# A recommendation tower on one core: dense layers with samples on partitions, last block in two groups, weight preparation moved

## The chip, the cores and the metric

The kernel runs on one core of one Trainium2 chip. The metric is the device time of one execution in microseconds (us). Engines: TensorE (PE in the rows; PEld its weight loads), VectorE (DVE), ScalarE (ACT), GpSimd (POOL), and the sync engine (SP), which here only issues transfers; "SPq", "ACTq" are the queues of these engines. All arithmetic is in float32.

## The reference, cut to what matters

For each of 512 samples 26 rows of 64 numbers are gathered from tables (`e`); `r_dense_t` is 512 x 256. EPS is 1e-5, NI is 33, gains and shifts are inputs.

```python
x = layer_norm(dense_t @ Wd.T, gd, bd)                          # 512 x 128
y = layer_norm(jnp.einsum('bnd,ed->bne', sparse_t, Ws), gs, bs) # 26 x 128 a sample
y = jnp.einsum('bne,pn->bep', y, Wsi)                           # 26 -> 32
y = layer_norm(y, gsi, bsi)
T = jnp.concatenate([x[:, None, :], jnp.swapaxes(y, 1, 2)], axis=1)   # 33 x 128
Z = jnp.einsum('bnd,bmd->bnm', T, T)
Zflat = Z[:, TRIL_I, TRIL_J]                                    # 528 a sample
out = layer_norm(Zflat @ Wl.T, gl, bl)                          # 512, first 384 kept
h = jnp.concatenate([z, r_dense_t], axis=1)
h = jnp.maximum(h @ W_top1 + b_top1, 0.0)                       # 640 -> 512
h = jnp.maximum(h @ W_top2 + b_top2, 0.0)                       # -> 256
y = h @ W_top3                                                  # -> 1
```

## The kernel before

**Tiling.** The 512 samples are four blocks of 128 (`BLOCKS`), each of four units of 32 samples (`BU`); 16 units in all. One step `step(t)` handles unit t. Each engine has its instructions in an order written out by hand; semaphores tie them together, and an engine that waits holds back all that stands behind the wait.

**A step.** GpSimd gathers the table rows (L257): 104 indirect transfers in a fixed order, two for each slot of `g_sb` (13 slots a block; a unit takes the next 4, 3, 3, 3 slots). On TensorE: `mix(t)` (L299) needs the scaled rows of unit t; `transposes(t + 1)` (L273) needs the gathered rows of unit t + 1; `project(t)` (L318) needs the copy `U` (ScalarE, L600, `keep_u`) of what mix made; `norms(t + 1)` (L284); `inner(t - 1)` (L333), the products of the 33 vectors. VectorE then adds the bias (L831), forms the norms of unit t + 1 and scales its rows (L802 to L824), which releases `mix(t + 1)`, and makes `T` (L850). ScalarE copies, squares, takes roots, and at the end of the step moves `psZ` to `Zs` in four pieces of 32 partitions (L639, `keep_z`), behind which stands the next `keep_u`.

**Layers behind a block.** When four units are in `Zs`, the sync engine moves them to `Zt` by seven transfers (`relay`, L214), so that 127 pairs lie on partitions, in 5 columns. The layers then have features on partitions: `linear` (L352) multiplies 4 x 5 weight tiles of 128 x 128 by `Zt` (128 samples), `variance` (L366) sums squares with a matrix of ones, `layer1` (L372) is 12 products, `layer2` (L409) 8, `output` (L417) 2. VectorE divides `psH` by the deviation and adds the part of layer 1 from the dense input, `hd` (L864 to L881). These are dealt to steps 6 to 15 (`LINEAR` is 6; `linear` is cut at `EARLY`). The last block's layers run behind step 15 (L424 to L469), its second half of `Zs` having been moved by seven transfers from the queues of SP, ScalarE and GpSimd.

**Weights.** `hd` for all 512 samples is 8 products of 512 columns (`dense_part`, L479): two parts before the first gathered rows are turned, the third before step 0, the fourth in step 0. The linear weights `wl` (1280 KB) are loaded once slot 3 is there (L226), summed on ScalarE in steps 1 and 2 (L749), scaled in steps 4 and 5 (L754); in steps 5 to 8 a bias is added to `hd` (L766).

## Time and profile before

| | us |
|---|---|
| time, median of 3 executions (lowest, highest) | 303.85 (299.91, 304.52) |
| span of the profiled execution | 185.4 |
| TensorE busy | 148.0 |
| VectorE busy | 130.1 |
| ScalarE busy | 106.9 |
| GpSimd busy (gathers) | 104.3 |
| mean granted clock of TensorE | 0.936 |

The time counts more than the span from the first to the last instruction: at the median 303.85 - 185.4 = 118.45 us lie around it. Busy times overlap, since the engines work side by side; which of them sets the pace has to be read step by step. The page's chain of waits, followed back from the last instruction, gives 40% of the span to TensorE, 23% to ScalarE, 19% to VectorE and 11% to issue.

### The profile page before, as it was taken

The numbers are of one execution on the slowest core, as the hardware profiler recorded it, in microseconds if no ns is written. First come the engines' busy times: TensorE is split into PE (matmuls) and PEld (weight loads), VectorE is DVE, ScalarE is ACT, GpSimd is POOL, SyncE is SP. The second block draws the span as 40 slices with busy tenths as digits, with TensorE's granted clock in tenths as the row PEclk, the third lists the DMA queues.
The fourth block names the chain that finished last, engine by engine and source line by source line (L and its number), as shares of the span: only waits on it lengthen the run. The fifth ranks groups of instructions, "written<-read, shape, count | busy, mean of one in ns | idle before, by whom it ended". The sixth has DMA issues, their size and how long they took to land.

```text
span 185.4 us, 4668 instructions
## 1 busy us (share of the span) xinstructions
PE 148.0 (80%) x1825; PEld 113.2 (61%) x1825; DVE 130.1 (70%) x300; ACT 106.9 (58%) x245; POOL 104.3 (56%) x111
## 2 busy tenths in 40 slices
PE   0089877977969947459996978899799799977995
PEld 0084544434549544419794947569596666877994
DVE  6269659772959594908697999579799967943142
ACT  1202435594868486866667877585877857831230
POOL 3778777877878777777777777777840000020000
PEclk9999999996999669855999999999999999997899
DMA  5816334141111112311111123111111100110000
GB/s 153 294 33 194 137 58 161 32 139 26 34 21 29 24 28 61 61 27 27 28 33 23 32 58 64 28 28 25 28 25 40 33 7 11 27 38 0 0 0 0
DMA packets 6003, 9.59 MB, mean 52 GB/s; under 512 B 2303, under 2 KB 3538, under 8 KB 5854
## 3 DMA queue, kind: packets, MB, share of 16 engines
q0 software_dynamic: 3392, 3.45, 10.3%
q1 hardware_dynamic: 2232, 5.08, 9.1%
q10 hardware_dynamic: 358, 0.78, 1.1%
q8 instruction: 14, 0.23, 0.5%
q14 instruction: 7, 0.06, 0.1%
HBM read 8.01 MB, written 0.00 MB: 43 GB/s over the span
## 4 chain that ended last, share of the span: by engine, by line
PE 40%; ACT 23%; DVE 19%; issue 11%; DMA 5%; ACTq 1%; DVEq 0%
PE psB L318 11%; ACT Zs L639 10%; DVE B L831 4%; ACT U L600 4%; DMA dense_sb<-in_dense 4%; PE psG L284 4%; DVE qA L809 4%; DVE prod L802 3%; PE psZ L333 3%; PE psW L352 3%; PE psU L299 3%; DVE ssB L838 3%; ACT sdB L617 2%; PE psB L520 2%; PE psZ L424 2%
## 5 line engine op out<-in xcount | busy, mean ns | idle before, releaser
L257 POOL DMA_INDIRECT g_sb<-in_table,row_id x104 | 102.8, 989 | 31.7 <-issue 31.4
L831 DVE TENSOR_TENSOR B<-psB,bias 128x512 f32<-128x512 f32 x31 | 20.0, 686 | 26.2 <-PE psB L318 26.2
L639 ACT ACTIVATE Zs<-psZ 32x264 f32<-32x264 f32 x59 | 36.3, 616 | 2.1 <-PE psZ L333 1.0
L318 PE MATMUL psB<-U,ws_g 64*128 64x512 f32 x64 | 20.9, 735 | 15.3 <-ACT U L600 15.2
L611 ACT ACTIVATE sqB<-B 128x512 f32<-128x512 f32 x31 | 19.1, 632 | 23.1 <-DVE B L831 23.1
L299 PE MATMUL psU<-wsi_x,g_sb 128*128 128x192 f32 (+4 forms) x128 | 23.3, 330 | 7.3 <-DVE g_sb L824 7.3
L299 PEld LDWEIGHTS psU<-wsi_x,g_sb 128*128 128x128 f32 x128 | 20.9, 206 | 11.1 <-DVE g_sb L824 11.0
L284 PEld LDWEIGHTS psG<-gram,sT 128*128 128x128 f32 x104 | 14.0, 207 | 14.5 <-ACT sT L587 10.0
L850 DVE TENSOR_TENSOR T<-B,rB 128x512 f32<-128x512 f32 x31 | 21.5, 692 | 1.1
L838 DVE TENSOR_REDUCE ssB<-sqB 128x16 f32<-128x512 f32 x32 | 21.7, 677 | 0.1
L284 PE MATMUL psG<-gram,sT 128*128 128x128 f32 x104 | 17.2, 308 | 0.7 <-ACT sT L587 0.7
L318 PEld LDWEIGHTS psB<-U,ws_g 64*128 64x128 f32 x64 | 5.4, 208 | 20.0 <-ACT U L600 20.0
L214 POOL DMA_DIRECT2D Zt<-Zs x2 | 1.1, 549 | 26.5 <-ACT Zs L639 26.5
L333 PE MATMUL psZ<-T 128*32 128x33 f32 x960 | 13.0, 202 | 0.3 <-issue 0.2
L333 PEld LDWEIGHTS psZ<-T 128*32 128x32 f32 x960 | 10.8, 112 | 3.3 <-issue 1.6
L352 PE MATMUL psW<-Zt,wl_g 127*128 127x128 f32 x100 | 12.8, 286 | 0.0
L352 PEld LDWEIGHTS psW<-Zt,wl_g 127*128 127x128 f32 x100 | 12.1, 199 | 0.5 <-issue 0.4
L600 ACT ACTIVATE U<-psU 128x512 f32<-128x512 f32 x16 | 9.5, 595 | 2.5 <-PE psU L299 2.2
L802 DVE TENSOR_TENSOR prod<-psG,g_sb 128x384 f32<-128x384 f32 (+1 forms) x16 | 9.3, 583 | 2.1 <-PE psG L284 2.1
L594 ACT ACTIVATE sdA<-qA,eps_c 128x6 f32<-128x6 f32 (+1 forms) x16 | 4.8, 300 | 9.5 <-DVE qA L812 9.0
L824 DVE TENSOR_TENSOR g_sb<-g_sb,rA 128x384 f32<-128x384 f32 (+1 forms) x16 | 9.5, 592 | 0.6
L809 DVE TENSOR_REDUCE qA<-prod 128x6 f32<-128x384 f32 (+1 forms) x16 | 9.4, 586 | 0.6
(159 smaller groups left out, 226.7 us busy)
## 6 DMA issues: line engine op xcount, KB each, us to landing
g_sb<-in_table,row_id POOLq DMA_INDIRECT x104, 2.5
wl_sb<-in_wl SPq DMA_DIRECT2D x1, 1280.0 KB, 6.0
w_sb<-in_w SPq DMA_DIRECT2D x2, 512.0 KB, 5.4
w_sb<-in_w SPq DMA_DIRECT2D x1, 768.0 KB, 4.5
small_sb<-in_small SPq DMA_DIRECT2D x1, 615.5 KB, 4.1
dense_sb<-in_dense ACTq DMA_DIRECT2D x1, 512.0 KB, 7.3
Zt<-Zs SPq DMA_DIRECT2D x3, 80.0 KB
Zt<-Zs SPq DMA_DIRECT2D x3, 70.0 KB
```

The source lines that it names most:

```text
L257: pool.indirect_dma_start(g_sb[:, k, h * DSP:(h + 1) * DSP], None, table, bass.IndirectOffsetOnAxis(row_id[:, 2 * k + h:2 * k + h + 1], 0) ...
L284: mm = pe.matmul(psG[:, n * P:(n + 1) * P], sT[:, u % 2, n * P:(n + 1) * P], gram[:, :], start=True, stop=True)
L299: mm = pe.matmul(psU[:, (lo - US * j) * PROJ:(hi - US * j) * PROJ], g_sb[:, SLOTS * b + c, :], wsi_x[:, c, lo - s0:hi - s0, :], start=(n = ...
L318: pe.matmul(psB[h][:, :], ws_g[h * DSP:(h + 1) * DSP, :], U[h * DSP:(h + 1) * DSP, u % 2, :], start=not (last and h == 0), stop=True).then ...
L333: mm = pe.matmul(bank[gq * PROJ:(gq + 1) * PROJ, n * COLS:(n + 1) * COLS], T[:, u % 2, h, s, 2:2 + PROJ], T[:, u % 2, h, s, 0:COLS], start ...
L352: mm = pe.matmul(bank[:, at * BS:(at + 1) * BS], wl_g[0:KL, jj, f * P:(f + 1) * P], Zt[0:KL, b, :, jj, :], start=(jj == 0), stop=(jj == CW ...
L600: act.activation(U[:, u % 2, :], psU[:, :], ACT.Copy).then_inc(U_ready, 1)
L611: act.activation(sqB[:, h, :], at, ACT.Square).then_inc(B_squared, 1)
L639: act.activation(to, product, ACT.Copy).then_inc(Z_kept, 1)
L831: dve.tensor_tensor(B[:, h, :].rearrange("p (s j) -> p s j", j=PROJ), psB[h][:, :].rearrange("p (s j) -> p s j", j=PROJ), bias[:, :].rearr ...
L838: dve.tensor_reduce(ssB[:, h, :], sqB[:, h, :].rearrange("p (s j) -> p s j", j=PROJ), AX, ALU.add).then_inc(B_summed, 1)
L850: dve.tensor_tensor(T[:, u % 2, h, :, 2:], at.rearrange("p (s j) -> p s j", j=PROJ), rB[:, h, :].rearrange("p (s o) -> p s o", o=1).broadc ...
```

## The change

Rows and lines of after are those of the changed kernel.

1. **Samples on partitions.** `linear`, layer 1 and layer 2 now take the activations as the stationary operand and stream the weights: 5 products of 512 columns, 3 of 512, 4 of 256. For this the activations are turned on TensorE twice (`turn_z`, 3 transposes; `turn_h`, 4), each behind a copy on ScalarE (`keep_zc`, `keep_zT`, `relu_h`). The squares are summed by the accumulator of the squaring itself (`square_z`), so `variance` goes; the deviation is one number a partition. VectorE computes h1 = hd x sd + product in one instruction (`add_h1`), likewise h2 (`add_h2`), multiplies by the last weights with an accumulator (in place of `output`), and divides at the end (`finish_y`).
2. **Last block as two groups of 64 samples.** A group's product is split by columns into two halves that write partitions 0 to 63 and 64 to 127 (`GROUPS`, g = 2); the halves are added by a product with `same_sb` (`fold`, `fold_y`). The first group's transfers start when units 12 and 13 are in `Zs`, the second's after unit 15, three from SP and four from GpSimd each (`SP_RELAYS`, `POOL_RELAYS`).
3. **Dense part.** One part for each block, in steps 4, 5, 9 and 13 (`HD_STEPS`), with its bias as a further product; each copy by ScalarE stands in the step behind it.
4. **Weights.** `wl` is loaded as soon as the dense input is there, and summed on ScalarE before step 0; it is scaled in steps 1 to 3. The first weights of layer 1 (768 KB) are loaded once slot 5 is there (before: slot 7), the dense ones (512 KB) once slot 8 is there (before: at the start). `late` (448 KB) is a new input, loaded after slot 14. The x part (`xn`, `xT`) moves behind the first unit's norms and into step 0.
5. **Output.** Five transfers of 4 bytes from each partition in place of one of 2 KB from one partition.

```diff
+HD_STEPS = (4, 5, 9, 13)
+GROUPS = ((0, 1), (1, 1), (2, 1), (LAST, 2), (LAST, 2))
```

SP's queue:

```diff
+            sp.wait_ge(d_dense, 16)
+            sp.dma_start(wl_sb[:, :, :], wl).then_inc(d_wl, 16)
+            sp.wait_ge(gathered[5], 32)
+            sp.dma_start(w1_sb[:, 0:KZ, :], w1[:, 0:KZ, :]).then_inc(d_w1, 16)
+            sp.wait_ge(gathered[8], 32)
             sp.dma_start(w1_sb[:, KZ:, :], w1[:, KZ:, :]).then_inc(d_w1d, 16)
-            sp.wait_ge(gathered[3], 32)
-            sp.dma_start(wl_sb[:, :, :], wl).then_inc(d_wl, 16)
```

TensorE: linear, the transposes, layer 1, the folding, and the step:

```diff
-            def linear(b, lo, hi):
+            def linear(k, lo=0, hi=CW):
...
-                for n in range(lo, hi):
-                    f, jj = n // CW, n % CW
-                    bank, at = (psW, f) if b < LAST - 1 else (psW_third[f // 2], f % 2)
-                    mm = pe.matmul(bank[:, at * BS:(at + 1) * BS], wl_g[0:KL, jj, f * P:(f + 1) * P],
-                                   Zt[0:KL, b, :, jj, :], start=(jj == 0), stop=(jj == CW - 1))
-                if hi == ALL or b == LAST - 1:
...
+                for jj in range(lo, hi):
+                    for n in range(g):
+                        mm = pe.matmul(psL[k][n * s:(n + 1) * s, 0:w], zt_of(k)[0:KL, jj, :], wl_g[0:KL, jj, n * w:(n + 1) * w],
+                                       start=(jj == 0), stop=(jj == CW - 1))
+                if hi == CW:
                     mm.then_inc(W_done, 1)
...
+            def turn_z(k):
+                g = GROUPS[k][1]
...
+                for c in range(KZ if g == 1 else 2):
+                    mm = pe.transpose(psQ[k][:, c * P:(c + 1) * P], zc[:, c * P:(c + 1) * P], eye_sb)
+                mm.then_inc(ztr_done, 1)
...
+                        mm = pe.matmul(psF[k][n * s:(n + 1) * s, 0:w], zT[:, place(c, g)],
+                                       w1_g[:, c, n * w:(n + 1) * w], start=(c == 0), stop=(c == KZ - 1))
+                if hi == KZ:
...
+            def fold(k):
+                pe.wait_ge(z_squared, k + 1)
...
+                pe.matmul(psS[k][:, 0:1], same_sb, ssq[:, k:k + 1], start=True, stop=True).then_inc(folded, 1)
...
                 mix(t)
+                if t == UNITS - 2:
+                    linear(b, 0, 2)
                 if t + 1 < UNITS:
                     transposes(t + 1)
+                if late_step and j == 1 and t < UNITS - 1:
+                    turn_z(b)
+                if late_step and j == 2:
+                    turn_h(b)
                 project(t)
                 if t + 1 < UNITS:
                     norms(t + 1)
-                if late and j == 1 and t < UNITS - 1:
-                    linear(b, EARLY[b], ALL)
+                else:
+                    turn_z(b)
                 if t:
                     inner(t - 1)
-                if t == UNITS - 1:
-                    linear(b, EARLY[b], ALL)
                 if t == 0:
-                    dense_part(3)
+                    x_part()
                 if t == 1:
+                    shift_part(0, 3)
+                if t == 2:
+                    shift_part(3, CW)
                     x_sum()
-                    shift_part(0, 2)
-                if t == 2:
-                    shift_part(2, CW)
                 if t == 3:
                     bias_part()
-                if late and j == 0:
-                    if b:
-                        output(b - 1)
-                    linear(b, 0, EARLY[b])
-                if late and j == 1 and t < UNITS - 1:
-                    variance(b)
-                if late and j == 2:
-                    layer1(b)
-                if late and j == 3:
+                if t in HD_STEPS:
+                    dense_part(HD_STEPS.index(t))
+                if late_step and j == 0:
+                    linear(b, 2 if t == UNITS - 2 else 0, CW)
+                if late_step and j == 1 and t < UNITS - 1:
+                    top1(b)
+                if late_step and j == 2:
                     layer2(b)
```

What stands behind the last step on TensorE in the changed kernel is shown by its order below. ScalarE, new functions and the step (keep_hd is dealt behind rows_out, the weights' scaling to the step's end):

```diff
+            def keep_zc(k):
+                n = FOUT if k < LAST else 2 * P
+                act.wait_ge(W_done, k + 1)
+                if k:
+                    act.wait_ge(ztr_done, k)
+                act.activation(zc[:, 0:n], psL[k][:, 0:n], ACT.Copy).then_inc(zc_ready, 1)
+
+            def square_z(k):
+                n = FLIN // GROUPS[k][1]
+                if k:
+                    act.wait_ge(z_squared, k)
+                act.activation(z_sq[:, 0:n], psL[k][:, 0:n], ACT.Square,
+                               accum_out=ssq[:, k:k + 1]).then_inc(z_squared, 1)
+
...
-            keep_hd(0)
-            keep_hd(1)
             rows_out(0)
-            act.wait_ge(x_tr, 1)
-            act.activation(xT[:, :], psB[0][:, :], ACT.Copy).then_inc(xT_ready, 1)
+            sum_wl(0, 2)
             deviation_a(0)
-            keep_hd(2)
+            sum_wl(2, CW)
...
+                late_step = 0 <= b < LAST
+                if late_step and j == 1:
+                    keep_zc(b)
+                    square_z(b)
                 keep_u(t)
...
+                if late_step and j == 1 and t < UNITS - 1:
+                    keep_zT(b)
+                if late_step and j == 2:
+                    relu_h(b)
+                if t - 1 in HD_STEPS:
+                    keep_hd(HD_STEPS.index(t - 1))
+                if t == 4:
+                    act.wait_ge(bz_done, 1)
+                    act.activation(bz[:, :], psH[0:1, :], ACT.Copy).then_inc(bz_ready, 1)
...
                 if t == 1:
+                    scale_wl(0, 2)
+                if t == 2:
+                    scale_wl(2, 3)
+                if t == 3:
...
+                    scale_wl(3, CW)
```

VectorE:

```diff
+                dve.scalar_tensor_tensor(out=h1[:, 0:n], in0=hd[:, b, at:at + n], scalar=sd[:, k:k + 1],
+                                         in1=psF[k][:, 0:n], op0=ALU.mult, op1=ALU.add).then_inc(h1_ready, 1)
+                dve.reciprocal(zr[:, k:k + 1], sd[:, k:k + 1]).then_inc(r_ready, 1)
...
+                dve.scalar_tensor_tensor(out=h2[:, 0:n], in0=b2, scalar=sd[:, k:k + 1], in1=psO[k][:, 0:n],
+                                         op0=ALU.mult, op1=ALU.add).then_inc(h2_added, 1)
+                dve.wait_ge(h2_added, k + 1)
+                dve.scalar_tensor_tensor(out=h2w[:, 0:n], in0=h2[:, 0:n], scalar=0.0, in1=w3, op0=ALU.max, op1=ALU.mult,
+                                         accum_out=y_part[:, k:k + 1]).then_inc(y_summed, 1)
```

**TensorE, step 6 from inner(5) on and step 7**, before (`L333` inner, `L352` linear, `L299` mix, `L273` transposes, `L318` project, `L284` norms, `L366` variance):

```order
L333 MATMUL psZ<-T 32x33 x32
L352 MATMUL psW<-Zt,wl_g 128x128 x9
L299 MATMUL psU<-wsi_x,g_sb 128x64
L299 MATMUL psU<-wsi_x,g_sb 128x192 x2
L299 MATMUL psU<-wsi_x,g_sb 128x160
L273 MATMUL psT<-small_sb,g_sb 128x128 x4
L318 MATMUL psB<-U,ws_g 128x512 x2
L284 MATMUL psG<-gram,sT 128x128 x4
L352 MATMUL psW<-Zt,wl_g 128x128 x11
L333 MATMUL psZ<-T 32x33 x32
L366 MATMUL psH<-z_sq,ones_sb 128x128 x4
```

and of the change (`L353` inner, `L379` linear, `L317` mix, `L291` transposes, `L392` turn_z, `L336` project, `L302` norms, `L411` layer 1):

```order
L353 MATMUL psZ<-T 32x33 x32
L379 MATMUL psW<-wl_g,Zt 128x512 x5
L317 MATMUL psU<-wsi_x,g_sb 128x64
L317 MATMUL psU<-wsi_x,g_sb 128x192 x2
L317 MATMUL psU<-wsi_x,g_sb 128x160
L291 MATMUL psT<-small_sb,g_sb 128x128 x4
L392 MATMUL psH<-small_sb,zc 128x128 x3
L336 MATMUL psB<-U,ws_g 128x512 x2
L302 MATMUL psG<-gram,sT 128x128 x4
L353 MATMUL psZ<-T 32x33 x32
L411 MATMUL psW<-w_g,zT 128x512 x3
```

All of linear now stands in step 6 ahead of mix(7), inner(6) comes ahead of everything else in step 7, and three transposes stand between transposes(8) and project(7).

**ScalarE, from the last roots of step 1 to the start of step 2**, before (`L617` roots, `L639` keep_z, `L743` and `L749` weights, `L600` keep_u, `L587` copy of the turned rows):

```order
L617 ACTIVATE sdB<-ssB,eps_c 128x16
L639 ACTIVATE Zs<-psZ 32x8x33
L743 ACTIVATE Zt<-psH,small_sb 2x8x64
L749 ACTIVATE wl_g,wl_sum<-wl_sb 128x512 x2
L600 ACTIVATE U<-psU 128x512
L587 ACTIVATE sT<-psT 128x384
```

and of the change (`L686` scaling, `L592` keep_u):

```order
L609 ACTIVATE sdB<-ssB,eps_c 128x16
L631 ACTIVATE Zs<-psZ 32x8x33
L686 ACTIVATE wl_g<-wl_sb,wl_off,gg 128x512 x2
L592 ACTIVATE U<-psU 128x512
L579 ACTIVATE sT<-psT 128x384
```

The two summing instructions and the copy into `Zt` left this place; two scaling instructions stand there.

**TensorE behind the last project**, before:

```order
L333 MATMUL psZ<-T 32x33 x32
L352 MATMUL psH<-Zt,wl_g 128x128 x10
L333 MATMUL psU<-T 32x33 x32
L366 MATMUL psG<-z_sq,ones_sb 128x128 x4
L372 MATMUL psB<-zT,w_g 128x128 x12
L397 MATMUL psW<-h1T,w_sb 128x128 x4
L424 MATMUL psZ<-Zt,wl_g 128x128 x5
L397 MATMUL psW<-h1T,w_sb 128x128 x4
L424 MATMUL psZ<-Zt,wl_g 128x128 x5
L424 MATMUL psT<-Zt,wl_g 128x128 x5
L424 MATMUL psU<-Zt,wl_g 128x128 x5
```

and of the change, from the last three weights' columns of block 2 on (`L411` layer 1, `L353` inner(15), `L379` linear of a group, `L420` turn_h, `L392` turn_z, `L433` layer 2, `L441` fold):

```order
L353 MATMUL psZ<-T 32x33 x32
L411 MATMUL psW<-w_g,zT 128x512 x2
L353 MATMUL psU<-T 32x33 x32
L411 MATMUL psW<-w_g,zT 128x512
L379 MATMUL psT<-wl_g,Zt 64x256 x10
L420 MATMUL psH<-small_sb,h 128x128 x4
L392 MATMUL psG<-small_sb,zc 128x128 x2
L433 MATMUL psW<-w_sb,h1T 128x256 x4
L441 MATMUL psZ<-ssq,late_sb 128x1
L411 MATMUL psT<-w_g,zT 64x256 x6
L379 MATMUL psB<-wl_g,Zt 64x256 x10
L420 MATMUL psG<-small_sb,h 128x128 x2
```

The first group's linear now stands ahead of block 2's second layer, and the second group's linear behind the first group's layer 1.

## Rows read from the trace of the kernel before

**Rows 1.** The page's 40 slices of 4.6 us: busy tenths of GpSimd, TensorE's granted clock.

```profile
POOL 3778777877878777777777777777840000020000
PEclk9999999996999669855999999999999999997899
```

**Rows 2.** GpSimd's gathers in the timeline; landings of those issued at 14 to 16.

```profile
20.84 0.94 POOL L257 DMA_INDIRECT g_sb<-in_table,row_id  x1 [0.30 <-issue]
...
136.35 0.94 POOL L257 DMA_INDIRECT g_sb<-in_table,row_id  x1 [0.30 <-issue]
...
DMA to landing us min/median/max: 5.2/5.3/5.5
```

**Rows 3.** The windows by step: stretch, length, busy us (instructions) per engine, clock, DMA.

```profile
25.77:32.83 7.06, 5.38 (x27) 3.08 (x26) 5.22 (x13) 3.76 (x9) 5.48 (x6) 1.00 0.50 139
32.83:42.21 9.38, 7.30 (x94) 3.62 (x92) 6.93 (x16) 7.20 (x17) 7.12 (x8) 1.00 0.32 83
70.83:80.87 10.04, 5.47 (x85) 4.08 (x85) 6.42 (x14) 7.84 (x17) 7.60 (x9) 0.81 0.25 52
132.75:140.05 7.30, 6.76 (x108) 5.85 (x109) 6.74 (x15) 5.09 (x12) 3.62 (x4) 1.00 0.13 25
155.40:183.81 28.41, 25.58 (x302) 22.71 (x301) 13.31 (x29) 10.34 (x26) 1.09 (x2) 0.94 0.05 12
```

**Rows 4.** ScalarE groups by line: shapes, count | busy us, mean ns | idle before.

```profile
L639 ACT ACTIVATE Zs<-psZ 32x264 f32<-32x264 f32 x59 | 36.3, 616 | 2.1 <-PE psZ L333 1.0
L754 ACT ACTIVATE wl_g<-wl_sb,wl_off,gg 128x512 f32<-128x512 f32 x5 | 3.6, 786 | 0.0
L749 ACT ACTIVATE wl_g<-wl_sb 128x512 f32<-128x512 f32 x5 | 3.1, 617 | 0.0
```

**Rows 5.** Timeline of TensorE: start, us, engine, line, operation, shape, count [idle before].

```profile
21.60 1.88 PE L479 MATMUL psW<-dense_sb,w_sb 128*128 128x512 f32 x4
...
145.76 1.36 PE L299 MATMUL psU<-wsi_x,g_sb 128*128 128x96 f32 x8 [0.39 <-DVE g_sb L824]
...
148.56 1.13 PE L318 MATMUL psB<-U,ws_g 64*128 64x512 f32 x4 [1.10 <-ACT U L600]
...
150.48 0.76 PE L333 MATMUL psZ<-T 128*32 128x33 f32 x64
...
151.62 2.50 PE L352 MATMUL psW<-Zt,wl_g 127*128 127x128 f32 x20
```

**Rows 6.** Timeline of TensorE, the first products and one step of the middle.

```profile
9.90 3.79 PE L520 MATMUL psB<-small_sb,dense_sb 128*128 128x128 f32 x16 [2.96 <-DMA dense_sb<-in_dense]
...
18.82 0.66 PE L273 MATMUL psT<-small_sb,g_sb 128*128 128x128 f32 x4
...
67.23 2.45 PE L299 MATMUL psU<-wsi_x,g_sb 128*128 128x128 f32 x8 [2.34 <-DVE g_sb L824]
```

**Rows 7.** Timeline behind the last step: all engines.

```profile
156.25 1.13 PE L318 MATMUL psB<-U,ws_g 64*128 64x512 f32 x4
...
162.23 1.26 ACT L639 ACTIVATE Zs<-psU 32x264 f32<-32x264 f32 x2
...
163.78 1.09 POOL L214 DMA_DIRECT2D Zt<-Zs  x2 [26.49 <-ACT Zs L639]
...
165.75 0.95 DVE L864 RECIPROCAL zr<-zsd 128x128 f32<-128x128 f32 x1 [2.31 <-ACT zsd L660]
...
166.74 0.42 DVE L898 TENSOR_TENSOR h<-psB,zr 128x256 f32<-128x256 f32 x1
```

**Rows 8.** The waits: who waited for whom, us in total, times, longest.

```profile
ACT sqB L611 <- DVE B L831: 23.1, 15, 2.5
```

**Rows 9.** The page's DMA issues: KB each, median us from issue to landing.

```profile
g_sb<-in_table,row_id POOLq DMA_INDIRECT x104, 2.5
wl_sb<-in_wl SPq DMA_DIRECT2D x1, 1280.0 KB, 6.0
...
w_sb<-in_w SPq DMA_DIRECT2D x1, 768.0 KB, 4.5
```

770 lines of the change are left out of this document (334 added, 436 removed).

## The prediction

> **What bounds the kernel now.** I read the 40 slices first, for TensorE's clock and for the engine that never rests. GpSimd works evenly to about 139 us and then stops: it issues 104 gathers one behind another [rows 1]. The 14th starts at 20.84 and the last at 136.35 [rows 2], so the 90 between them take 115.5 us, 1.283 each. A unit needs 6 or 8 of them, 8.3 us a step on average. This is the floor of the loop, since nothing touches these gathers.
>
> Then the windows by step, cut where ScalarE begins the copy U of each unit [rows 3]. From U(0) at 25.77 to U(15) at 155.40 lie 15 steps, 129.6 us, 8.64 each. The quickest with four pieces of Z takes 7.30 (step 12), step 1 takes 9.38, step 5 10.04. So the loop runs close to the gathers but behind them: the last gather, landed near 136.35 + 2.5 = 138.9 [rows 2, 9], is used behind mix(14), which ends at 147.1 [rows 5], 8 us late.
>
> Which wait ends last in a step? ScalarE has one queue: its four pieces of Z (616 ns each) and the roots stand ahead of the next U [rows 4]. In step 12 they fill the 7.30 exactly. What is added behind them adds to the step: two summing instructions in step 1 (617 ns plus their readout), three in step 2, scalings of 786 in steps 4 and 5, a bias instruction of about that length in each of steps 5 to 8 [rows 4]. That is why steps 1 to 5 are long. TensorE needs from the end of a U copy: project, norms and inner (148.56 to 151.24, 2.7 us), then what is dealt to the step, X, then mix 1.36 and the copy 0.6, so 4.7 + X [rows 5]. The third limit is the chain through VectorE, 7.06 in step 0 [rows 3].
>
> TensorE's clock is granted in full except from about 55 to 88 us [rows 1]; at half clock mix takes 2.45 where it takes 1.36 [rows 5, 6], and step 5 was granted 0.81 [rows 3].
>
> Behind U(15) come 28.4 us to the last VectorE instruction [rows 3]. I call p the start of the last project (156.25). Z is all copied at p + 7.24 (162.23 + 1.26), the transfers' issue on GpSimd ends 1.4 later [rows 7], the last instruction ends at 183.81 = p + 27.6 [rows 3].
>
> **The change part by part.** *Product shapes.* Two products of 512 columns take 1.88 us with their latency, so about 0.86 each at full clock; ten products of 128 take 2.50, or 0.23 each with latency [rows 5]. Linear: 20 x 0.22 = 4.4 becomes 5 x 0.86 = 4.3. Layer 1: 12 x 0.22 = 2.6 becomes 3 x 0.86 = 2.6. Layer 2 stays at 1.7. The shape alone gives nothing. It drops variance (4 x 0.22) and output (2 x 0.15, one weight column each) and adds seven transposes (0.66 for four with latency [rows 6], 0.15 each, 1.1). The seven lie between mix and project, where TensorE waits for the U copy anyway: 0.65 of wait against 0.5 of unit transposes plus 0.5 (turn_z) or 0.6 (turn_h), so about 0.4 of each reaches the chain, half of it hidden by ScalarE.
>
> *ScalarE.* Steps 1 to 5 lose 5 summings, 4 bias instructions in steps 5 to 8, and the second layer's two relus (0.62 in all) ahead of U. Sums go to the time before step 0, where ScalarE is idle. What comes in, the copies and relus of samples on partitions, stands either during mix (keep_zc and the squaring, 0.5 + 0.6 + 0.2 against 1.36) or behind rows_out, where ScalarE waits for VectorE's add (15 waits, 23.1 us, 1.5 each [rows 8]), at no cost while this wait is there; without it each would cost 0.6 a step.
>
> *Start.* The 1280 KB load took 6.0 us to land and the gathers issued beside it 5.3 instead of the usual 2.5 [rows 2, 9]. Now it runs from about 9.9 (when the first products waited for the dense input [rows 6]) to 16, and gather 8, which starts at 12.0, lands near 16. Turned rows, norms and scaling then take 5.5 (18.82 [rows 6] to 24.4, where mix(0) ends at U(0), less 1.36), so mix(0) starts near 21.5 instead of 24.4. But then unit 1 waits: the 768 KB load (4.5 to land) is now issued near 20.4, just ahead of gather 14 at 20.84, which I let land at 25.2, not 23.3. I also take away the dense products that kept TensorE busy there (such as the two at 21.60 [rows 5]), so it idles twice for some 2.5 us before 25. The first products of the kernel ran at 3.79/16 = 0.24 each, twice the 0.12 of the later ones [rows 5, 6], and I assume this half clock lasts through step 0. It costs 1.0 on project, 1.0 on mix, 0.3 on transposes: 2.3. U(1) = 25.2 + 0.5 + (7.06 - 0.65) + 2.3 = 34.4, against 32.83.
>
> *Steps, from U to U.* ScalarE decides 1 to 5, TensorE the steps with linear:
>
> - step 1: 7.3 + two scalings 1.6 = 8.9; step 2: 7.3 + 0.8 = 8.1; step 3: 7.3 + 0.1 + 0.7 (x into Zt, now here) + 1.6 = 9.7; step 4: 8.1; step 5: 7.3, since a dense part of three products (2.6) gives 4.7 + 2.6 = 7.3 too. U(6) = 76.5, against 80.87.
> - step 6: linear whole, 4.7 + 4.3 = 9.0; step 7: 7.3 + 0.5 for turn_z + 0.3 for the root of the deviation = 8.1; step 8: 7.5; step 9: 7.3. Steps 10 to 13 repeat them: 31.9 for each four. U(14) = 76.5 + 63.8 = 140.3.
> - step 14: two linear products (1.7) stand between mix(14) and the transposes, so project(14) starts at 140.3 + 1.7 + 0.4 = 142.4, and U(15) = 142.4 + 6.4 = 148.8.
>
> Against 155.40 that is 6.6 earlier. The gathers' floor is at 138.9 + 0.5 + 6.4 = 145.8, so the loop cannot win more than 9.6.
>
> *Behind the loop,* counted from p (now 148.8 + 0.65 = 149.5). A group's product is 256 columns on half the array's columns; two halves side by side take 0.43 if they overlap. The inner products do overlap: 64 instructions of 33 columns on 32 array columns take 0.76 us, 12 ns each, where 128 columns alone take 0.12 us [rows 5]. I take it for 64 columns too; ends: 0.43 a pair and 0.86. VectorE on 128 x 256 takes 0.42 [rows 7]; I use it for ScalarE on the same shape. Z all copied p + 7.2, as before, since two layer 1 products ahead of inner(15) lie in the wait for T. TensorE then: last layer 1 product and the first group's linear (5 x 0.43) to 9.0; six transposes 9.9; layer 2 of block 2 to 12.0 behind its relu; layer 1 of group 1 (1.3) 13.4. Four transfers from GpSimd at 0.55 each, where two took 1.09 [rows 7], land at 11.4, hidden. Linear of group 2 to 15.6; copy and transposes 16.5; layer 2 of group 1 (0.85) 17.4; layer 1 of group 2 18.7; folding, root and add 19.6; transposes and relu 20.5; layer 2 21.4; two VectorE instructions, folding and last product 22.6. The reciprocal of 128 x 128 (0.95 [rows 7]) is gone from this chain. So p + 22.6 = 172.1 against 183.81; with the 1.6 to the end of the span, 173.7 against 185.4.
>
> The Trainium skill, TensorEngine Tiling (Array Packing), Key Properties, says that changing the tiling mode drains TensorE. In the rows project, which uses 64 rows, follows transposes of full height and starts within 0.05 us of the U copy's end [rows 5], so by the rows a switch costs under 0.1 and the tail's dozen switches about 1 us at most; by the rule each would wait for the product ahead of it, about 0.2, and the time would be near 294.5.
>
> *Output.* Four of the five transfers lie under other work. The last has 64 rows of 4 bytes; I leave the 1.6 as it is, ends 1.0 and 2.5.
>
> **Sum.** The loop gives 6.6 and the tail 27.6 + 0.8 - 22.6 - 0.65 = 5.1, together 11.7; 185.4 - 11.7 = 173.7 of span, and with 118.45 around it 292.2. The runs shown spread from 299.91 to 304.52, so a median of the new one may lie 2 us off for that alone.
>
> **The rivals.**
>
> - *The clock stays up at the start* (before, the clock fell around mixes that had waited 2.3 us [rows 6], but not at each such wait). Then 2.3 less, and the loop ends near the gathers: 289 to 290. Chance 0.2.
> - *The clock falls in the middle again.* Seven tenths of a step is TensorE work once dense parts fill steps 4 and 5, against 5.47 of 10.04 in step 5 before [rows 3], which speaks against it. If it does as before, about 1.5 us in each of three steps: 296.7. Chance 0.13. The Trainium skill, TensorE: Matmul & The Clock Gate, Part 4, says that transposes do not count as busy in the same way; by it the fourteen products replaced by transposes would speak for this rival.
> - *The halves of a group do not overlap.* Then 0.43 becomes 0.86 in linear, layer 1 and layer 2 of both groups: (5 + 3 + 2) x 0.43 x 2 = 8.6, and 2.6 in step 13: 300.8 to 303, no change. The 32-column tiles speak against it. Chance 0.1.
> - *Slower:* half clock from step 6 to the end, if waits for gathers leave gaps. Every step then takes twice its TensorE part, 2 x (4.7 + 4.3) = 18 with linear and 13 to 15 in the others, over 40 us in all. It decides once more than 11.7 us are lost, three steps. The slices 20 to 40 were granted in full with the same kind of waits [rows 1]. Chance 0.03.
>
> **How the numbers follow.** The forecast's own case holds 0.54. Its steps are sums of idle-free pieces, and small stalls between them make later ends likelier than earlier ones. The range 287 to 299 holds the forecast, both clock rivals and the spread of runs, and leaves the overlap rival, the slower one and some low runs out, 0.2. A measurement of this kernel can tell about 2% from no change. Faster by over 2% is below 297.8: 0.84; within 2% 0.13; slower 0.03.
>
> **What would show it.** In the new profile: U(1) not earlier than before, at 33 to 35, behind gather 14; steps 1 to 5 of 8 to 9.7 with scalings ahead of U; steps 6 and 10 near 9, linear ahead of mix; U(15) at 146 to 150; waits for g_sb landings in the loop short; pairs in the groups' linear at 0.43; the last VectorE instruction 22 to 24 behind the last project. Wrong would be: mix over 2 us in the middle, pairs of 0.86, or a wait of project for the transposes that costs more than 0.5 in steps 7 and 11.

## The result, and the profile after

| | before | changed |
|---|---|---|
| time, median of 16 executions each | 303.62 (297.60 to 305.38) | 305.73 (304.94 to 307.71) |
| ratio | | 1.020, 95% interval 1.017 to 1.024 |
| span of the profiled execution | 185.4 | 305.1 |

The ratio is taken from the fast executions of each kernel alone; the medians of all 16 lie 0.7% apart. The forecast was 292.2, in a range from 287 to 299. By that ratio the changed kernel is 2% slower, and not 4% faster.

The second thing to see is the span. In the changed kernel the profiled execution took 306.97 and its span 305.1: 2 us lie around it, not 118. The span of 185.4 and the time near 304 of before do not belong to the same kind of execution. The runs below met six chips. On two of them (numbered 12 and 2) the kernel before takes 297 to 305, on four (7, 8, 11, 4) 182 to 189. Each comparison below is therefore between kernels that ran one after the other on one chip, unless it says otherwise. Each chip was met on one occasion only, so whether the chip makes the difference or something about the occasion is open; "chip" below stands for both.

The page of the changed kernel, engines and 40 slices (of 7.6 us each); [rows 1] are those of before:

```profile
PE 157.1 (51%) x1668; PEld 94.0 (31%) x1668; DVE 125.2 (41%) x301; ACT 105.9 (35%) x248; POOL 104.2 (34%) x117
PE   1720402300000302210598399999899988998960
POOL 5777777777777777740000000000000000022000
PEclk9955655555555555555589789999999999999995
```

TensorE's busy time is about that of before, but hardly any of it lies in the first 19 slices (to 145 us). Half clock alone would double it, not spread 19 us of work over 134. GpSimd works as before and stops in the 18th slice (134 us). The windows (us, busy time and instructions per engine, clock, DMA share, GB/s), from the start of this stretch to its end, then to U(15), then to the end of the span:

```profile
15.00:149.00 134.00, 19.39 (x87) 13.36 (x86) 14.71 (x38) 10.32 (x26) 90.42 (x95) 0.51 0.19 41
156.20:271.95 115.75, 103.16 (x1244) 59.65 (x1242) 85.12 (x187) 79.25 (x183) 0.69 (x2) 0.97 0.04 10
271.95:305.10 33.15, 20.83 (x266) 13.02 (x265) 10.10 (x28) 9.87 (x28) 3.41 (x7) 0.89 0.06 11
```

A product stands in the trace as two matmul instructions (the 32 products of an `inner` are the `x64` of [rows 5]). In 134 us TensorE starts 87 of them, some 44 products, and U(0) and U(1) are all that comes out. Behind the stretch, from U(2) at 156.20, 13 steps take 115.75 us, 8.9 each. What happens inside it is in the timeline (start, duration, engine, line, operation, count, idle before):

```profile
48.91 0.60 ACT L592 ACTIVATE U<-psU 128x512 f32<-128x512 f32 x1 [16.57 <-remote]
49.56 2.08 PE L336 MATMUL psB<-U,ws_g 64*128 64x512 f32 x4 [14.90 <-issue]
...
62.91 0.69 DVE L821 TENSOR_TENSOR B<-psB,bias 128x512 f32<-128x512 f32 x1 [29.77 <-remote]
63.63 0.63 ACT L603 ACTIVATE sqB<-B 128x512 f32<-128x512 f32 x1 [5.83 <-issue]
69.21 0.69 DVE L821 TENSOR_TENSOR B<-psB,bias 128x512 f32<-128x512 f32 x1 [5.61 <-remote]
...
139.24 0.21 PE L353 MATMUL psZ<-T 128*32 128x33 f32 x1 [0.50 <-issue]
143.45 0.22 PE L353 MATMUL psZ<-T 128*32 128x33 f32 x1 [4.00 <-issue]
145.55 0.22 PE L353 MATMUL psZ<-T 128*32 128x33 f32 x1 [1.88 <-issue]
146.25 0.22 PE L353 MATMUL psZ<-T 128*32 128x33 f32 x1 [0.48 <-issue]
...
149.07 0.70 PE L353 MATMUL psZ<-T 128*32 128x33 f32 x32 [0.50 <-issue]
```

TensorE answers ScalarE's copy of U within 0.05 us (48.91 + 0.60 to 49.56), and ScalarE answers VectorE's B as quickly (62.91 + 0.69 to 63.63). Only what comes out of TensorE is late: the two products issued at 49.56 are there for VectorE at 62.91 and 69.21, where at half clock they take 2.08 in all. The matmul instructions of 33 columns then stand alone, 0.70 us apart or a multiple of it, until at 149.07 the last 32 of them start within 0.70. VectorE and ScalarE have their usual durations (B 687 ns against 686 on the page of before, Zs 614 against 616 [rows 4]).

The record of the stretch is itself thin. Of the semaphore updates that transfers make when they land, the trace of the changed kernel holds 20 to 34 in each 20 us from 20 to 140 us; the trace of the same kernel without a stretch (chip 8, below) holds 224 to 299. So the page can give no time to landing for the gathers, first here and then on chip 8, and many waits of the stretch are put down to "remote":

```profile
g_sb<-in_table,row_id POOLq DMA_INDIRECT x104
g_sb<-in_table,row_id POOLq DMA_INDIRECT x104, 2.4
```

### The profile page after: what moved, and what is told of

It reads as the page before. It is cut to its first block, busy times and chain, and to the rows that moved or that the text cites. A ratio compares the mean times of both kernels' runs of the same rounds, so it can differ in the third digit from the quotient of the medians.

```text
span 305.1 us, 4377 instructions
## 1 busy us (share of the span) xinstructions
PE 157.1 (51%) x1668; PEld 94.0 (31%) x1668; DVE 125.2 (41%) x301; ACT 105.9 (35%) x248; POOL 104.2 (34%) x117
## 4 chain that ended last, share of the span: by engine, by line
PE 33%; issue 22%; another core or an unknown queue 21%; DVE 12%; ACT 8%; DMA 1%; SPq 0%; DVEq 0%; ACTq 0%
PE psB L336 6%; PE psU L317 4%; ACT Zs L631 4%; PE psW L379 4%; PE psH L462 3%; DVE B L821 3%; PE psZ L353 2%; DVE qA L799 2%; PE psG L302 2%; DVE prod L792 2%; ACT U L592 2%; PE psH L472 2%; PE psW L480 2%; PE psW L411 1%
## 5 line engine op out<-in xcount | busy, mean ns | idle before, releaser
L275 POOL DMA_INDIRECT g_sb<-in_table,row_id x104 | 99.7, 958 | 31.7 <-issue 31.4
L228 POOL DMA_DIRECT2D Zt<-Zs x8 | 4.1, 521 | 144.3 <-ACT Zs L631 137.2
L317 PE MATMUL psU<-wsi_x,g_sb 128*128 128x192 f32 (+4 forms) x128 | 23.6, 332 | 51.1 <-DVE g_sb L814 51.1
L317 PEld LDWEIGHTS psU<-wsi_x,g_sb 128*128 128x128 f32 x128 | 21.3, 207 | 61.4 <-DVE g_sb L814 57.4
L336 PE MATMUL psB<-U,ws_g 64*128 64x512 f32 x64 | 20.0, 703 | 38.3 <-issue 33.6
L592 ACT ACTIVATE U<-psU 128x512 f32<-128x512 f32 x16 | 9.5, 596 | 47.3 <-remote 36.9
L302 PE MATMUL psG<-gram,sT 128*128 128x128 f32 x104 | 18.2, 320 | 13.8 <-issue 13.8
L302 PEld LDWEIGHTS psG<-gram,sT 128*128 128x128 f32 x104 | 14.8, 217 | 27.1 <-issue 18.8
L353 PE MATMUL psZ<-T 128*32 128x33 f32 x960 | 14.1, 201 | 16.9 <-issue 16.9
L336 PEld LDWEIGHTS psB<-U,ws_g 64*128 64x128 f32 x64 | 5.2, 200 | 42.6 <-issue 34.9
L353 PEld LDWEIGHTS psZ<-T 128*32 128x32 f32 x960 | 11.4, 112 | 19.9 <-issue 18.3
L579 ACT ACTIVATE sT<-psT 128x384 f32<-128x384 f32 (+1 forms) x16 | 8.2, 512 | 19.0 <-issue 7.8
L379 PE MATMUL psW<-wl_g,Zt 128*128 128x512 f32 x30 | 13.8, 603 | 0.0
L291 PE MATMUL psT<-small_sb,g_sb 128*128 128x128 f32 x52 | 9.9, 297 | 1.9 <-DMA g_sb<-in_table,row_id 1.8
L411 PE MATMUL psW<-w_g,zT 128*128 128x512 f32 (+1 forms) x30 | 10.2, 520 | 1.0 <-ACT zT L652 1.0
```

What stands on the lines that cost most here:

```text
L275: pool.indirect_dma_start(g_sb[:, k, h * DSP:(h + 1) * DSP], None, table, bass.IndirectOffsetOnAxis(row_id[:, 2 * k + h:2 * k + h + 1], 0) ...
L302: mm = pe.matmul(psG[:, n * P:(n + 1) * P], sT[:, u % 2, n * P:(n + 1) * P], gram[:, :], start=True, stop=True)
L317: mm = pe.matmul(psU[:, (lo - US * j) * PROJ:(hi - US * j) * PROJ], g_sb[:, SLOTS * b + c, :], wsi_x[:, c, lo - s0:hi - s0, :], start=(n = ...
L336: pe.matmul(psB[h][:, :], ws_g[h * DSP:(h + 1) * DSP, :], U[h * DSP:(h + 1) * DSP, u % 2, :], start=not (last and h == 0), stop=True).then ...
L353: mm = pe.matmul(bank[gq * PROJ:(gq + 1) * PROJ, n * COLS:(n + 1) * COLS], T[:, u % 2, h, s, 2:2 + PROJ], T[:, u % 2, h, s, 0:COLS], start ...
L379: mm = pe.matmul(psL[k][n * s:(n + 1) * s, 0:w], zt_of(k)[0:KL, jj, :], wl_g[0:KL, jj, n * w:(n + 1) * w], start=(jj == 0), stop=(jj == CW ...
```

## Experiments

### Is the stretch new, and what makes it

Four kernels on chip 12, where before took 298.29.

The kernel before, unchanged. 

> The kernel before, unchanged, for a second trace. Theory S (both kernels have the slow stretch in timed executions, the profile on record of before is an execution without it): a span near 300, within 3 us of its time, with TensorE products that take 5 to 8 times their duration from about 15 us until 10 to 20 us behind the last gather, and about 13 steps of 7 to 10 us after it. Theory N (the stretch is new in the changed kernel, and before has a constant 118 us outside its span): a span of 184 to 187 beside a time near 303.

The gathers replaced (the other rows are why its output isn't the reference's):

```
-                    pool.indirect_dma_start(
-                        g_sb[:, k, h * DSP:(h + 1) * DSP], None, table,
-                        bass.IndirectOffsetOnAxis(row_id[:, 2 * k + h:2 * k + h + 1], 0),
-                    ).then_inc(gathered[k], 16)
+                    pool.dma_start(g_sb[:, k, h * DSP:(h + 1) * DSP],
+                                   table[P * (2 * k + h):P * (2 * k + h + 1), :]).then_inc(gathered[k], 16)
```

> The changed kernel, with each of the 104 gathers replaced by a plain transfer of 128 consecutive rows of the table from the same queue; the samples therefore get other rows than the reference's. Theory G (the slow stretch of TensorE lasts while GpSimd issues gathers by index): no stretch, steps of 7 to 9 us from the start, span 165 to 185. Theory Q (any transfer that GpSimd issues does it): the stretch lasts until 10 to 20 us behind the last such transfer, which at 0.55 us each is near 70 us, span 215 to 240. Theory W (the stretch has a length of its own, once TensorE has idled or changed clock): it ends near 149 as before, span near 305.

Products without a reader, `filler(n)` being n products of 512 columns into `psB[1]`, at four places ahead of mix(0):

```
+            pe.wait_ge(fill_ready, 1)
+            filler(6)
             pe.wait_ge(d_small, 16)
...
+            filler(3)
             transposes(0)
+            filler(1)
             norms(0)
+            filler(4)
```

> The changed kernel with 14 products of 512 columns whose result nobody reads, ahead of TensorE's waits: 6 before the first operand has landed, 3 before the first transposes, 1 before norms(0), 4 before mix(0), so that it never idles for long in the first 25 us. Theory W (the stretch begins because TensorE idled around 12 to 17 us): no stretch, or a much shorter one, span 175 to 195. Theory G or Q: the stretch begins in the same place and ends near 149, span 305 or a few us more.

Forty gathers more, behind the 104:

```
+            for n in range(MORE):
+                pool.indirect_dma_start(
+                    more_sb[:, n, :], None, table,
+                    bass.IndirectOffsetOnAxis(row_id[:, n:n + 1], 0),
+                ).then_inc(d_extra, 16)
```

> The changed kernel with 40 more gathers behind the 104, whose rows nobody reads; by 1.25 us each GpSimd then issues until about 184 instead of 134. Theory G or Q: the stretch of slow products lasts some 50 us longer, to about 200, so about six steps fewer lie behind it; two or three more steps are done slowly in it, and the span is 330 to 355. Theory W: the stretch ends near 149 and the span stays at 305 within 3.

| kernel | time | span | U(2) at | U(15) at |
|---|---|---|---|---|
| before | 301.69 | 299.9 | 159.33 | 269.88 |
| changed, plain rows | 187.56 | 185.7 | 36.97 | 153.53 |
| changed, filler products | 304.79 | 303.0 | 155.55 | 270.82 |
| changed, 40 more gathers | 361.60 | 359.8 | 211.80 | 327.59 |

The slices of before on this chip, and two windows (15 to 148.6, then from U(2) to U(15)):

```profile
PE   0740610300002600040097793769788999899697
POOL 5777777777777777760000000000000000000100
PEclk9985575555555655555579979779999999999989
```

```profile
15.00:148.60 133.60, 22.94 (x65) 13.70 (x63) 15.84 (x48) 7.56 (x17) 90.57 (x95) 0.55 0.18 43
159.33:269.88 110.55, 90.24 (x1346) 71.08 (x1347) 87.35 (x186) 80.28 (x182) 0.00 (x0) 0.95 0.05 11
```

Each of these is one execution. Theory S holds, N falls: the kernel before has the same stretch of the same length. W falls: keeping TensorE at work ahead of mix(0) changed nothing. The gathers by index cause it (G, not Q): with plain transfers from the same queue, the same bytes and the same shapes, it is gone. (The plain transfers also read consecutive rows and are all issued by 60 us; which part of a gather by index matters is not separated.) And it lasts as long as they do: 40 more of them, 50 us of GpSimd, put U(2) 56 us later. The span of 359.8 lies above the 330 to 355 expected for this run: in the longer stretch too only two units were done. There the single matmul instructions go on past the last gather, which starts near 183, and then recover:

```profile
187.14 0.21 PE L362 MATMUL psZ<-T 128*32 128x33 f32 x1 [2.59 <-issue]
...
199.74 0.21 PE L362 MATMUL psZ<-T 128*32 128x33 f32 x1 [2.59 <-issue]
...
204.64 0.21 PE L362 MATMUL psZ<-T 128*32 128x33 f32 x1 [1.18 <-issue]
205.34 5.13 PE L489 MATMUL psW<-wl_sb,am 128*34 128x512 f32 x6 [0.49 <-issue]
```

So on such a chip a kernel does about two units until 16 to 22 us behind the last gather, and the rest at full pace. Whatever is gained inside the stretch is given back at its end: U(0) came at 48.91 in the changed kernel and at 89.11 in before, U(2) at 156.20 and 159.33.

One rival no run tests. All executions on record were recorded by the hardware profiler, and the record is thin just where TensorE is slow: 675 landing updates in the whole trace of before here and 804 in that of the changed kernel, against 2363 with plain rows on this chip and 2266 with gathers on chip 8. Gathers and recording together may be what holds TensorE, and whether the stretch is there in an execution that nobody records is open.

### How dense the gathers have to be

A paced kernel, with a fill of 128 x 512 on GpSimd behind each gather, and one in which every second gather is plain (its half of the rows is not the reference's). The first runs, the paced kernel on chip 7 and the half plain one on chips 7 and 8 (before 184.0 and 186.27), met no stretch.

```
+                    pool.memset(pace_sb[:, :], 0.0).then_inc(paced, 1)
+                    pool.wait_ge(paced, 2 * k + h + 1)
```

> The changed kernel with a fill of 128 x 512 on GpSimd behind each gather, which sets the gathers some 0.6 us further apart, so that they last until about 200 instead of 134. Theory P: the same 104 gathers take the same from TensorE, but leave it more time between them, span 300 to 312. Theory H: TensorE runs at nearly full pace between them, and the gathers set the end: U(15) near 210, span 240 to 250. Theory L: the stretch lasts until about 215, with one or two steps more done in it, and span 345 to 365.

> The changed kernel, in which every second gather (the second 64 columns of each slot) is a plain transfer of consecutive rows; 52 gathers by index stay, one every 1.8 us instead of 1.25, and half of the input is not the reference's. Theory P (each gather by index takes about 1.15 us from TensorE, wherever it stands: 305.1 less 185.7 over 104): span 240 to 250. Theory H (TensorE is held only while gathers follow one another closely): steps run at nearly full pace between them, span below 215. Theory L (TensorE stays slow for as long as gathers go on, at any density): the stretch lasts until about 110, and 14 steps with the tail follow, span 255 to 275.

> The changed kernel with every second gather plain (half of the input is not the reference's). On a chip of the second kind this is within 2 us of 187.4 of span, as in the last call. On one of the first kind, theory P (each gather by index takes 1.15 us from TensorE): span 240 to 250. Theory H (only gathers that follow one another closely do it): below 215. Theory L (slow for as long as gathers go on): 255 to 275.

Spans 231.7, 187.4 and 184.4: nothing told of the stretch, only that spaced gathers bound the loop, the last one starting at 187.8. Then on chip 2, where before took 300.62:

> The changed kernel with a fill of 128 x 512 on GpSimd behind each gather (the last gather then starts at 188 instead of 133). On a chip with the slow stretch, theory P: the same 104 gathers take the same from TensorE, 300 to 312. Theory H: span 232 to 250, as on a chip without the stretch (231.7). Theory L: the stretch ends near 205, span 345 to 365. On a chip without it: 231.7 again, nothing told.

> The changed kernel with every second gather plain (half of the input is not the reference's). On a chip with the slow stretch, theory P (each gather by index takes 1.15 us from TensorE): span 240 to 250. Theory H (only gathers that follow one another closely do it): below 215. Theory L (slow for as long as gathers go on): the stretch ends near 110 to 115, span 255 to 275. On a chip without it: 184 to 188, nothing told.

Times 233.53 and 191.70. The pages' slices, first of the paced kernel, then of the half plain one:

```profile
PE   0814573889381998988769597967985999799930
POOL 4888888888888888888888888888888860321000
PEclk9965557699857799999997978895899799999965
```

```profile
PE   0592948979539898999979899997989996999720
POOL 4888888888888888888882000000000012120000
PEclk9997599999966999999999999999999999999955
```

Neither has a stretch, on the chip and occasion on which before and two further versions (below) have it: the paced kernel has the very span (231.7) that it has on chip 7. Theories P and L fall, H holds. All 104 gathers are there in the paced kernel, so it is no price for each; they hold TensorE while one follows another every 1.25 us, and not at one each 1.79. Even so the traces of this chip lack landing updates: 1791 in the paced kernel (2285 on chip 7) and 1497 in the half plain one (2308 on chip 8). On chip 2 the paced kernel takes 0.78 of the time of before (one execution); on a chip without the stretch it is 27% slower than before.

To find the spacing between, I took the version of the next section with shorter fills, from the ninth gather on:

> The version with both edits, and from the ninth gather on a fill of 128 x 128 on GpSimd behind each gather, which sets one gather each 1.4 us or so (1.25 without). Theory K (on chips with the stretch a gather and what TensorE issues share something that takes about 1.4 us a gather, so the queue only grows when gathers come faster than that): the last gather starts near 150, U(15) near 160, no stretch or a short one, time 188 to 200 against 300 of before. Theory H2 (the limit lies nearer to 1.8): the stretch is there in full, 310. On a chip without the stretch: the gathers bound the loop, time 187 to 191.

> The same with a fill of 128 x 256 behind each gather, one gather each 1.5 to 1.6 us. The last starts near 163, U(15) near 172, span 200, time 202 on either kind of chip if 1.55 us is far enough apart; near 320 on a chip with the stretch if it isn't.

> The version with both edits and a fill of 128 x 128 behind each gather from the ninth on. On a chip without the stretch 194, as in the last call (before 186.5). On one with it, theory K: no stretch or a short one, 192 to 200 against 300 of before, ratio 0.64 to 0.67; theory H2 (the limit is nearer to 1.8 us): the stretch in full, 305 to 315.

All three met chips without the stretch (11, 11 and 4; before 186.5 each time): 194.03, 203.08 and 192.91, the last at a ratio of 1.048 (1.030 to 1.067). They tell the price there: at one gather each 1.44 us 11 to 13 us over the 181 to 182 that the same version takes without fills on other chips (below), where 187 to 191 had been expected. The limit between 1.25 and 1.79 they leave open.

### What the change does without the stretch

Before with plain rows, on chip 7. 

> The kernel before, with each of the 104 gathers replaced by a plain transfer of 128 consecutive rows (other rows than the reference's), to stand beside the changed kernel with the same replacement, 185.7 of span. If the change as such gained what was forecast, before is 11 to 12 us longer: 197. If it gained nothing apart from the gathers, before is within 3 us of 185.7; no gathers hold the first units back, so 180 to 185 is what I expect, with U(15) to the end 30 us.

Span 184.9, against 185.7 of the changed kernel with the same rows (one execution each, the other on chip 12): nothing of the 11.7 us forecast shows.

The changed kernel itself, on chip 8. 

> The changed kernel, unchanged. The runs so far fall into two kinds by the chip they ran on: before took 298 to 305 on some and 183 to 187 on another. If this chip is of the first kind: 304 to 307, ratio to before 1.01 to 1.025. If it is of the second, where the trace on record of before belongs too: from the steps of the run with plain rows (span 185.7) I expect 186 to 189 against 183 to 187 of before, ratio 1.005 to 1.03. The forecast would have put it at 174 + 2 = 176, ratio 0.95.

Median 193.56 against 186.27, ratio 1.037 (1.018 to 1.056). The 186 to 189 expected came from the run with plain rows, in which no gather holds the start back: it had U(15) at 153.53, this one at 158.60. The span of the profiled execution is 191.6, where my working gives 173.7. Now both traces are of one kind, and the steps can be held against [rows 3] and the forecast. The windows of steps 1, 3, 7, 8 and 14, then from U(15) to the last VectorE instruction:

```profile
32.80:42.34 9.54, 8.58 (x94) 4.17 (x92) 7.87 (x22) 6.57 (x14) 7.26 (x8) 0.86 0.29 82
50.30:65.86 15.56, 9.85 (x94) 4.02 (x95) 7.85 (x18) 7.71 (x17) 11.90 (x13) 0.78 0.14 25
91.26:98.99 7.73, 7.73 (x100) 4.92 (x98) 5.75 (x12) 5.77 (x14) 5.89 (x7) 1.00 0.13 27
98.99:107.64 8.65, 6.89 (x98) 4.99 (x97) 6.75 (x15) 5.77 (x13) 6.52 (x8) 1.00 0.15 29
149.05:158.60 9.55, 9.55 (x97) 5.07 (x95) 6.17 (x14) 6.74 (x16) 0.69 (x2) 1.00 0.01 3
158.60:184.17 25.57, 21.08 (x266) 13.14 (x265) 10.09 (x28) 9.88 (x28) 3.41 (x7) 0.96 0.08 14
```

Step 3 takes 15.56 instead of 9.7, and the span ends 7.4 us behind the last VectorE instruction instead of 1.6. The timeline of step 3, and from the waits that of SyncE's queue at the end (us in total, times, longest):

```profile
58.43 0.34 ACT L759 ACTIVATE Zt<-psH,small_sb 2x128 f32<-2x128 f32 x1
...
58.92 4.67 PE L472 MATMUL psH<-w_sb,small_sb 128*1 128x512 f32 x6 [5.05 <-ACT Zt L759]
...
63.52 1.01 PE L473 MATMUL psH<-bs_sb,one_r 1*1 1x512 f32 x2
```

```profile
SPq L75 <- DMA out_y<-y_all: 6.5, 1, 6.5
```

`bias_part` waits for `x1_ready`, which ScalarE gives behind all four pieces of Z of step 3. TensorE idles 5.05 us, its granted clock falls to half, and the first four of the six instructions of 512 columns (two to a product) start 0.85 us apart instead of 0.43, with mix(4) queued behind. And the last output, 64 runs of 4 bytes, keeps the queue waiting 6.5 us.

Both can be mended in a few lines. The outputs of each of the last two groups are folded into a row of one partition, the reciprocal going into the folding weights ahead of time; ScalarE copies x into Zt at the start of step 3:

```
+                    dve.tensor_scalar(same_z[:, k - LAST, :], same_sb[:, 0:PS], zr[:, k:k + 1], None,
+                                      ALU.mult).then_inc(same_scaled, 1)
...
-                pe.matmul(psS[k][0:PS, 0:1], same_sb[:, 0:PS], y_part[:, k:k + 1], start=True,
+                pe.matmul(psS[k][0:1, 0:PS], y_part[:, k:k + 1], same_z[:, k - LAST, :], start=True,
...
+                if t == 3:
+                    act.wait_ge(x1_done, 1)
...
                 squares_b(t, 0)
                 squares_b(t, 1)
```

On chip 7: 

> The changed kernel with two edits. (1) The two last groups' 64 outputs are folded into one row of one partition, with the reciprocal of the deviation put into the folding weights ahead of time, and leave as one run of 256 B instead of 64 runs of 4 B. (2) ScalarE copies the sums of x into Zt at the start of step 3 and no longer at its end, so that bias_part does not wait. My theory: the last VectorE instruction to the end of the span falls from 7.8 to about 1.7 us (-6), U(3) to U(4) from 16.4 to 10 or 11 (-6), time 293 to 295, ratio to before 0.965 to 0.98. Rival for (1): the end waits for something else than the shape of the transfer and stays at 7 to 8, then 299. Rival for (2): bias_part is slow by itself (6.3 us for four products) and only the wait of 5.1 goes, or the next step takes the gain back, then 296 to 299.

On chip 8, beside the changed kernel: 

> The version with the row of outputs and x copied early, again, beside the changed kernel on the same chip. On a chip of the second kind: 181, ratio 0.98 to 0.99, and 6 below the changed kernel if both edits do as much as their places in the trace say less what runs into the gathers. On one of the first kind: 293 to 295, ratio 0.965 to 0.985, since both places lie behind the stretch of slow products, where nothing of the gathers is left.

On chip 2: 

> The version with the row of outputs and x copied early. On a chip with the slow stretch: 293 to 295, ratio to before 0.965 to 0.985, since both places lie behind the stretch. Rival there: the stretch ends 12 us later in it by some coupling, and nothing is gained (305). On a chip without it: 181 to 182, ratio 0.98 to 0.99, as twice before.

The row of outputs alone, on chip 2: 

> The changed kernel with the row of outputs alone; x is copied at the end of step 3 as there. From the last VectorE instruction to the end of the span 1.7 instead of 7.8 us, U(3) to U(4) stays at 15.5 to 16.5. Time 5.5 to 6.5 above the version with both edits and 5.5 to 6.5 below the changed kernel: 187 to 188 on a chip without the stretch, 299 on one with it. Rival: what the early copy of x gives in step 3 was lost anyway in a later wait for gathers, and both versions take the same.

| kernel | chip | time | ratio to before (95%) |
|---|---|---|---|
| both edits | 7 | 181.15 | 0.986 (0.976 to 0.995) |
| both edits | 8 | 181.89 | 0.983 (0.970 to 0.996) |
| both edits | 2 | 293.78 | 0.975 (0.967 to 0.984) |
| row alone | 2 | 299.38 | 0.998 (0.995 to 1.002) |
| changed kernel | 8 | 193.56 | 1.037 (1.018 to 1.056) |

The windows of step 3 and from U(15) to the last VectorE instruction, with both edits on chip 8, and SyncE's wait:

```profile
50.46:59.44 8.98, 8.08 (x96) 3.84 (x95) 7.92 (x18) 7.50 (x17) 6.85 (x8) 1.00 0.12 22
151.82:177.72 25.90, 21.34 (x266) 13.07 (x265) 10.72 (x30) 9.88 (x28) 3.42 (x7) 0.95 0.07 14
```

```profile
SPq L75 <- DMA out_y<-y_row: 0.8, 1, 0.8
```

Step 3 falls by 6.6, the end by 5.9 (7.4 to 179.2 - 177.72 = 1.5): 12.5, where the span fell by 12.4 and the time by 11.7. That is twice the 6 us that I had expected between the two versions on chip 8. Chip 2 parts the edits: 5.6 between the row alone and both, about 6 between the row alone and the changed kernel's 305.7, which comes from other executions. My theory of both places held, and neither rival did. The version with both edits is faster than before on all three chips, each interval below 1, by an amount about as large as the 2% that can be told from no change. It is also faster than the changed kernel, though on a chip with the stretch the two never ran on one occasion.

## Why the prediction was wrong

**The frame.** The first step that failed is the one sentence "span 185.4 + 118.45 around it". Nothing lies around the span but 2 us; the 118 are a stretch in which TensorE hardly works, and in an execution that has it the steps that I costed against the gathers do not exist. I had seen that 118 us had no row in the trace, and took them as a constant. The first 15 us and steps 0 and 1, where I spent half of the working, count for nothing there. The first question should have been which execution the median belongs to, and no row of the one trace could answer it.

This step is not what put the forecast out of its range. Around the span of 191.6 that the changed kernel has without the stretch, 118.45 would give 310.1, and 305.73 were measured: as a constant it was right within 5 us, by luck, since the same stretch stands in both kernels. What failed in number is the sum. From U(2) to the end of the span my working has 130.4 us (173.7, less U(2) at 34.4 + 8.9 = 43.3); the trace of the result has 148.9, and the one without the stretch 149.3. The same terms failed in both, above all the wait of `bias_part` in step 3, which I put at nothing (5.9 us), and the last output, taken over at 1.6 (7.4 without the stretch). For the two kernels with the stretch this comes to 8.3 us more behind U(2) (148.9 against 140.6), less 3.1 by reaching U(2) earlier. I had given slower a chance of 0.03, and no rival named either place.

**The sum, on a chip without the stretch** (193.56 measured, 191.6 of span, 173.7 in my working; 17.9 missed):

- *Start, U(1) at 34.4:* 1.6 too late, 32.80. The third transpose of unit 1 waited for its gather until 24.40 (I had 25.2). Step 0 ran at half clock, project 2.08 instead of 1.13, as assumed, but not for my reason: the first products of before, from which I took it, took 0.24 each while the clock was granted in full [rows 1]. In the changed kernel too the clock was full until 12 us and at half from 16 on, behind waits of 0.8 to 1.2 us for gathers. So the half clock was right by luck.
- *Steps ScalarE decides:* steps 1, 2, 4 measured 9.54, 7.96, 8.00 against 8.9, 8.1, 8.1. Close.
- *Step 3:* 15.56 against 9.7, 5.9 missed. I priced the copies into Zt on ScalarE at 0.7 and never asked who waits for them. `bias_part` on TensorE did, with mix(4) behind it. With the wait gone the step takes 8.98.
- *Steps with linear:* step 6 took 9.12 and step 10 9.27, against 9.0. Right. From 73.86 to 158.60 us, steps 5 to 14, the granted clock was 1.00, and the one fall in the middle, in step 3, came with the wait that I had not seen: the rival of a falling clock is out.
- *Steps 8 and 12:* 8.65 and 8.67 against 7.5. I put the cost of the transposes ahead of project at 0.6; in step 8 it is 1.35, since they wait for h1, which VectorE computes only behind the last half of T of the step before: T ends at 99.68, `h` at 100.34, and project starts at 100.98, not at 99.63 right behind the copy U. I had named a wait above 0.5 as what would be wrong, for steps 7 and 11; it came one step later. Step 7 took 7.73 against 8.1.
- *Step 14:* 9.55 against 8.5; the steps 5, 9 and 13 lost 0.6 to 1.0 each. These small stalls and the two of 1.15 make 5.5, and step 3 the other 5.9; the start gave back 1.6, so U(15) came at 158.60, 9.8 behind my 148.8.
- *Tail, last VectorE instruction at p + 22.6:* p + 24.9 (159.25, 184.17). The halves overlap, as assumed: the two of a pair start 0.01 us apart, and five products of 256 columns in two halves each take 2.38 us with their latency, 0.43 for both halves of a product. That rival is out. The 2.3 built up over the chain's handovers, 0.4 by the copies of Z, 1.2 by layer 2 of the first group.
- *Output:* 1.6 taken over from before, with ends of 1.0 and 2.5; measured 7.4. I took the row of another transfer (one run of 2 KB) for 64 runs of 4 bytes, and the upper end from nothing at all. This one term is a third of what was missed. The Trainium skill, DMA: Bandwidth & Descriptors, Specifications, puts the size from which a transfer reaches line rate at 512 B. Which side of 512 B a run lies on does not tell its price here: one run of 256 B, also below it, kept the queue waiting 0.8 us and 64 runs of 4 B 6.5. Whether the number of the runs or their length costs this is not separated.

So the mechanisms on which I spent the rivals (clock, overlap, mode switch) behaved as forecast, though two of the readings behind them were weak. The clock is told above. For the mode switch I read a project that had waited 1.10 us for the copy U [rows 5], a wait that would have hidden a drain. The tail of the changed kernel has the switch without a wait: transposes start 0.31 us behind the last halves, where halves follow each other at 0.21, so 0.1 a switch stands.

Two things that I had given one line each, a moved copy and a reshaped output, took 5.9 + 5.8 = 11.7 us, as much as the forecast gain. With both mended the change gains 1.4 to 2.5%; of the span's 17.9 us 5.5 remain (179.2 against 173.7), the small stalls and the tail less what the start came earlier. Their causes are read from the one trace, and no run takes them away.

## What to carry to other kernels

If a kernel's time and its profiled span do not agree, find out what lies between before costing anything: run it once more and look at the span of a run that has the time. Where its trace has far fewer semaphore updates than another of the same kernel, ask whether the recording takes part in what it shows. For each instruction that a change moves later, list the waits of every engine on its semaphore, and what is queued behind them. Price a transfer by its shape (how many runs, how long), by the last row of that shape only.

## What the hardware showed

- On two of six chips, each met on one occasion, TensorE's products end late while gathers by index from GpSimd follow each other every 1.25 us. TensorE's matmul instructions stand at multiples of 0.70 us, in the run with more gathers mostly 2.80 apart, where two make a product of 33 columns. VectorE and ScalarE keep their durations, and SyncE's loads behind the same gathers go out at 19.64, 27.13, 35.21 and 42.62 us, against 19.94, 27.81, 37.08 and 43.28 without the stretch. Plain transfers of the same shape from the same queue, GpSimd busy 0.54 us with each, do not do it, nor do gathers 1.79 us apart. It begins 12 to 25 us behind the first gather (norms(0), issued at 17.22, is late in the changed kernel, while with 40 more gathers U(0) still came at 23.93), and ends 16 to 22 us behind the last (133.1 to 149.1, 183.2 to 205.3). What is shared, whether the recording of the execution takes part, why only some chips or occasions show it and where between 1.25 and 1.79 us the limit lies, stays open; a version with 1.44 never met such a chip.
- An idle gap of 5.05 us on TensorE cost 1.9 us more in the products behind it, most of which ran at half clock (5.6 against 3.7 us for the same eight matmul instructions of `bias_part`).
